# Second-layer keys and values of context batches 2 and 3 made inside the second layer, from a context loaded again

## The reference, cut to what matters

```python
# first layer, on the normed context, with rotation and a bias
kv_in = _layernorm(encoder_output, gamma, beta)
k = kv_in @ Wqkv[D:2*D].T ;  v = kv_in @ Wqkv[2*D:].T ;  q, k = rope(q), rope(k)
attn = softmax(q @ k.T * SCALE + temporal_bias);  attended = attn @ v      # then out, gate, tanh FFN
# second layer, on the raw context
k = ctx @ wk.T + bk ;  v = ctx @ wv.T + bv
attn = softmax(where(mask == 0, -1e9, q @ k.T * 8 ** -0.5)) ;  out = attn @ v   # then wo, 8 experts, top 2
```

## Time and profile before

| what | value |
|---|---|
| median of 3 runs | 558.69 us (555.54 to 559.5) |
| profiled execution | 558.84 us, its span 557.2 us |
| PE busy | 508.0 us (91%), 6338 matmuls |
| ACT busy | 434.7 us (78%) |
| DVE busy | 280.2 us (50%) |
| POOL busy | 169.0 us (30%) |
| mean granted TensorE clock | 0.977 |
| DMA | 74.53 MB, mean 134 GB/s |
| chain that ended last | PE 53%, ACT 12%, DVE 10%, issue 9%, POOL 8%, DMA 5% |

### The profile page before, as it was taken

How to read it: one execution, slowest core, us unless ns; L and a number is a source line. 1 busy time by engine, 2 the same in 40 slices (tenths; PEclk the granted TensorE clock), 3 DMA queues, 4 the chain that set the end, 5 groups by cost and what they waited for, 6 DMA issues and landing times.

```text
span 557.2 us, 15361 instructions
## 1 busy us (share of the span) xinstructions
PE 508.0 (91%) x6338; PEld 260.7 (47%) x6338; DVE 280.2 (50%) x739; ACT 434.7 (78%) x496; POOL 169.0 (30%) x202
## 2 busy tenths in 40 slices
PE   7788998999899898998999999899899989998995
PEld 4444545445445454554555444344443444443343
DVE  5858566874776356653522342336243533440354
ACT  1257486787678787888998999899989998999832
POOL 4468637584785308840110001000000000000000
PEclk9789899999899999999999999999999999999996
DMA  8579885389558314580745291249123910000000
GB/s 269 160 230 288 225 273 138 129 283 292 148 192 285 124 49 126 197 261 17 140 105 188 69 211 40 87 113 223 33 65 76 235 32 8 6 1 2 6 6 16
DMA packets 51584, 74.53 MB, mean 134 GB/s; under 512 B 11146, under 2 KB 40050, under 8 KB 51506
## 3 DMA queue, kind: packets, MB, share of 16 engines
q1 hardware_dynamic: 40258, 37.54, 26.9%
q0 software_dynamic: 5632, 24.07, 12.9%
q10 hardware_dynamic: 5616, 11.86, 7.0%
HBM read 39.95 MB, written 18.83 MB: 106 GB/s over the span
## 4 chain that ended last, share of the span: by engine, by line
PE 53%; ACT 12%; DVE 10%; issue 9%; POOL 8%; DMA 5%; ACTq 1%; SPq 1%; DVEq 0%; POOLq 0%
PE ps L539 24%; PE ps L515 16%; ACT probs L1171 7%; DVE k_swapped L1480 2%; DMA q_side<-in_far_q 2%; PE ps L669 2%; ACT ctx_turned L1171 2%; PE ps L440 2%; DMA ctx_tokens<-in_ctx_rows 2%; DVE row_stats L1442 1%; POOL k L1025 1%; PE ps L450 1%; ACT ctx_tokens L1171 1%; DVE k_parts L1497 1%; POOL k L1023 1%
## 5 line engine op out<-in xcount | busy, mean ns | idle before, releaser
L1171 ACT ACTIVATE probs<-ps 124x1024 f32<-124x1024 f32 (+1 forms) x305 | 295.7, 1024 | 54.2 <-PE ps L520 41.1
L515 PE MATMUL ps<-q_side,k_side 64*124 64x256 bf16 (+1 forms) x1664 | 159.9, 291 | 20.9 <-ACT probs L1171 12.1
L539 PE MATMUL ps<-probs,values 124*9 124x256 f32 (+1 forms) x2440 | 163.7, 383 | 0.0
L515 PEld LDWEIGHTS ps<-q_side,k_side 64*124 64x124 bf16 (+1 forms) x1664 | 80.0, 131 | 124.7 <-ACT probs L1171 62.0
L539 PEld LDWEIGHTS ps<-probs,values 124*9 124x9 f32 (+1 forms) x2440 | 52.9, 90 | 65.6 <-issue 15.5
L1054 POOL TENSOR_TENSOR post_rstd<-post_rstd,power 128x2 f32<-128x2 f32 x12 | 8.5, 712 | 194.0 <-DVE post_rstd L1695 126.5
L520 PE MATMUL ps<-bias_near,bias_w 64*124 64x84 bf16 (+1 forms) x416 | 42.5, 200 | 0.0
L1171 ACT ACTIVATE ctx_tokens<-ps 124x1024 f32<-124x1024 f32 (+1 forms) x37 | 37.9, 1026 | 4.9 <-PE ps L515 4.0
L1480 DVE SCALAR_TENSOR_TENSOR k_swapped<-ps,beta_products,k_table_sb 32x496 f32<-32x496 f32 (+2 forms) x64 | 40.4, 632 | 0.9
L1171 ACT ACTIVATE ctx_turned<-ps 124x1024 f32<-124x1024 f32 (+1 forms) x37 | 37.9, 1024 | 3.4 <-PE ps L515 2.4
L1171 ACT ACTIVATE ctx_normed<-ps 124x1024 f32<-124x1024 f32 (+1 forms) x37 | 37.9, 1025 | 2.4 <-PE ps L515 1.6
(11 more groups left out here) (256 smaller groups left out, 621.0 us busy)
## 6 DMA issues: line engine op xcount, KB each, us to landing
k_side<-k_scratch SPq DMA_DIRECT2D x24, 400.2 KB, 7.8
k_scratch<-k_parts POOLq DMA_DIRECT2D x16, 372.0 KB, 5.4
k_side<-k_parts SPq DMA_DIRECT2D x45, 124.0 KB, 2.5
q_side<-q_parts SPq DMA_DIRECT2D x63, 64.0 KB, 2.7
v_scratch<-values POOLq DMA_DIRECT2D x4, 936.0 KB, 10.9
values<-v_scratch SPq DMA_DIRECT2D x4, 936.0 KB, 14.4
v_scratch<-v POOLq DMA_DIRECT2D x12, 288.0 KB, 5.8
mask_q<-in_mask POOLq DMA_DIRECT2D x8, 400.5 KB, 4.4
```

Of the source, the lines that this page charges most:

```text
L515: last = pe.matmul(ps[0:width, bank, SQ * i:SQ * (i + 1)], kst[rows, j % 2, 2 * g + i, at], qst[rows, query_slot(j, run), 2 * g + i, :], s ...
L539: last = pe.matmul(ps[32 * i:32 * i + VC, ACC + g // 2, SQ * (g % 2):SQ * (g % 2) + SQ], v[0:rows, j % 2, t, h, :], probs_of(u)[0:rows, SQ ...
L1171: act.activation(probs_of(u)[0:rows, :], ps[0:rows, s:s + 2, :].rearrange("p a n -> p (a n)"), ACT.Exp)\
```

## The change

For context batches 2 and 3 (`LATE_FROM` = 2) attention batches 1 and 2 make only the layer-1 keys and values. Each chunk then has one value step, of up to four tiles, in HIGH, and VectorE rounds the high key part before it takes the values out. The layer-2 keys and values of these two batches are made in attention batches 4, 5 and 6, at the slots of `second_keys_at`, from a context that ScalarE's queue loads again (`load_turned_again`, 800 KB, at units (3, 12) and (5, 19)). All of their rounding is VectorE's; SP stores them and loads them back: the keys in two parts, the last chunk's part behind its own store. `VALUES_AT` is changed for batches 4, 5 and 6 (batch 7 keeps the default), two expert steps move from slots 20 and 22 to 22 and 24, and the exps' fifth buffer is the layer-1 key buffer and no longer the turned context.

```diff
+LATE_FROM = 2
+def key_steps(b, n):
+    return KEY_STEPS[n] if b < LATE_FROM else 2
...
+def second_keys_at(j, slot):
+    chunks = {NB: {32: (4, "k1v1"), 36: (5, "k1"), 40: (5, "v1"), 48: (6, "k1"), 50: (6, "v1")},
+              NB + 1: {14: (3, "k1"), 16: (3, "v1"), 28: (4, "k1v1"), 32: (5, "k1"), 36: (5, "v1"), 48: (6, "k1"), 50: (6, "v1")},
+              NB + 2: {14: (3, "k1"), 16: (3, "v1")}}
...
-             NB: (2, 0, 3, 3, 0, 3, 3, 0, 3, 1, 3, 0, 3, 1, 3, 2, 3, 2, 3, 2, 2, 0, 3, 1, 3, 3)}
+             NB: (2, 0, 3, 3, 0, 3, 3, 0, 3, 1, 3, 0, 3, 1, 3, 2, 2, 2, 2, 2, 1, 1, 3, 2, 3, 4),
+             NB + 1: (2, 0, 3, 3, 1, 0, 3, 2, 1, 3, 3, 2, 2, 2, 2, 2, 1, 1, 1, 2, 3, 2, 3, 2, 2, 4),
+             NB + 2: (2, 0, 3, 3, 1, 0, 3, 2, 1, 3, 3, 2, 3, 1, 3, 1, 3, 0, 3, 1, 3, 1, 3, 1, 3, 3)}
...
-    steps = (8, 10, 20, 22, 34, 38, 42, 46)
+    steps = (8, 10, 22, 24, 34, 38, 42, 46)
...
+                    if b >= LATE_FROM:
+                        return
                     fill(HIGH, "k1", b, n)
...
+                elif b >= LATE_FROM:
+                    fill(HIGH, "v", b, n)
+                    one_layer_values(HIGH, n, 0).then_inc(made[HIGH], 1)
...
+            def one_layer_values(bank, n, layer):
+                for i, t in enumerate(range(*CHUNKS[n])):
+                    r = rows_of(t)
+                    last = pe.matmul(ps[0:r, bank, D * i:D * i + D], ct[:, TS * t:TS * t + r], wvv[:, layer, :], start=True, stop=True)
+            def second_layer_keys(b, n, what):
+                pe.wait_ge(ct_late_in, 16 * (b - LATE_FROM + 1))
+                if "k1" in what:
+                    fill(HIGH, "k1", b, n)
+                    pe.matmul(ps[:, HIGH, 0:k_1 - k_0], wk1[:], ct[:, k_0:k_1], start=True, stop=True).then_inc(made[HIGH], 1)
+                if "v1" in what:
+                    fill(LOW, "v1", b, n)
+                    one_layer_values(LOW, n, 1).then_inc(made[LOW], 1)
...
 # SP, in batches 5 and 6, for the batch after
-                    load_second_keys(j + 1, range(len(TERMS)))
+                    if j == NB:
+                        load_second_keys(j + 1, range(len(TERMS)))
+                    else:
+                        store_late(j - NB + 1, 2)
+                        load_late_keys(j + 1, 0)
+                        store_late(j - NB + 1, 3)
+                        load_late_keys(j + 1, 1)
                     load_second_values(j + 1)
+                    if j < NJ - 2:
+                        store_late(j - NB + 2, 0)
...
                 load_shift(j + 1)
+                if NB <= j < NJ - 2:
+                    store_late(j - NB + 2, 1)
...
 # VectorE
             def rest_of_keys(b, n):
+                if b < LATE_FROM: ...
+                else:
+                    high_part(b, n)
+                    first_layer_values(b, n)
                 middle_part(b, n)
...
 # in choose(b), after the third gate step
+                if later:
+                    second_layer_keys(*later)
+                    second_layer_values(*later)
...
 # in the loop over batches 3 to 7
+                    if j < NJ - 1:
+                        second_layer_parts(j - NB + 1, 3)
                 if looks:
                     look_at_mask(looks[1])
+                later = j - NB + 2 if NB <= j < NJ - 2 else None
                 if j < NJ - 1:
-                    for c in range(2):
-                        sample_maxima(j + 1, c)
+                    sample_maxima(j + 1, 0)
+                    if later:
+                        second_layer_keys(later, 0)
+                        second_layer_values(later, 0)
+                        second_layer_parts(later, 0)
+                    sample_maxima(j + 1, 1)
+                    if later:
+                        second_layer_keys(later, 1)
                     make_shift(j + 1)
+                    if later:
+                        second_layer_values(later, 1)
+                        second_layer_parts(later, 1)
...
                     weigh(j - NB - 1, 1)
+                if later:
+                    second_layer_keys(later, 2)
+                    second_layer_values(later, 2)
                 copy_sums(j)
+                if later:
+                    second_layer_parts(later, 2)
```

More of the change, by code:

```diff
@@ L113, in keys_at @@
     for at, (b, n) in first.items():
-        if slot - at in KEY_OFFSETS[:KEY_STEPS[n]]:
+        if slot - at in KEY_OFFSETS[:key_steps(b, n)]:
             return b, n, KEY_OFFSETS.index(slot - at)
     return None
+def second_keys_at(j, slot):
+    chunks = {NB: {32: (4, "k1v1"), 36: (5, "k1"), 40: (5, "v1"), 48: (6, "k1"), 50: (6, "v1")},
+              NB + 1: {14: (3, "k1"), 16: (3, "v1"), 28: (4, "k1v1"), 32: (5, "k1"), 36: (5, "v1"), 48: (6, "k1"), 50: (6, "v1")},
+              NB + 2: {14: (3, "k1"), 16: (3, "v1")}}
+    if slot not in chunks.get(j, {}):
+        return None
+    m, what = chunks[j][slot]
+    return *divmod((j - NB + 1) * NC + m, NC), what
 def sample_at(j):
@@ L686, in beside @@
                     keys(*keys_at(j, slot))
+                if second_keys_at(j, slot) is not None:
+                    second_layer_keys(*second_keys_at(j, slot))
                 if j + 1 < NJ and slot in sample_at(j):
@@ L843, in load_second_keys, with load_late_keys, store_late @@
                 load_keys(sp, G, 1, b, j % 2, k1_in, terms)
+            def load_late_keys(j, half):
+                b = j - NB
+                sp.wait_ge(k1_in, QL * (b + half))
+                if half and b > LATE_FROM:
+                    sp.wait_ge(k1_rest_in, QL * (b - LATE_FROM))
+                for s in range(2):
+                    sp.wait_ge(k1_late_out[s], 16 * (2 * (b - LATE_FROM) + max(half, 1 - s) + 1))
+                cut = CHUNK_KEYS[3][0]
+                load_keys(sp, G, 1, b, j % 2, (k1_in, k1_rest_in)[half], keys=((0, cut), (cut, SK))[half])
+            def store_late(b, n):
+                m, s = late_chunk(b, n), n % 2
+                (t0, t1), (k_0, k_1) = CHUNKS[n], CHUNK_KEYS[n]
+                if m >= 2:
+                    sp.wait_ge(k1_late_out[s], 16 * (m // 2))
+                    sp.wait_ge(v1_late_out[s], 16 * (m // 2))
+                sp.wait_ge(seen[LOW], side.of(LOW, "v1", b, n))
+                sp.dma_start(G["v_dram"][1, b, :, t0:t1], v1s[:, s, 0:t1 - t0]).then_inc(v1_late_out[s], 16)
+                sp.wait_ge(lo1, NC * b + n + 1)
+                sp.dma_start(G["k_dram"][1, b, :, :, k_0:k_1], kp1[:, s, :, 0:k_1 - k_0]).then_inc(k1_late_out[s], 16)
             def load_second_values(j):
@@ L1310, in scalar_program @@
                     key = keys_at(*divmod(u - lag, UB))
-                    if key is not None and key[2] == 0:
+                    if key is not None and key[2] == 0 and key[0] < LATE_FROM:
                         part(*key[:2])
@@ L1525, in both_values, with first_layer_values @@
                 last.then_inc(seen[bank], 1)
+            def first_layer_values(b, n):
+                t0, t1 = CHUNKS[n]
+                if n == 0:
+                    dve.wait_ge(probs_used, UB * (b - 1))
+                    dve.wait_ge(v0_out, 16 * (b - 1))
+                dve.wait_ge(made[HIGH], side.of(HIGH, "v", b, n))
+                for p0, p1 in ((t0, t1),) if t1 < KT else ((t0, KT - 1), (KT - 1, KT)):
+                    r, nt = rows_of(p1 - 1), p1 - p0
+                    at = D * (p0 - t0)
+                    product = ps[0:r, HIGH, at:at + D * nt].rearrange("p (t h d) -> p t h d", h=H, d=HD)
+                    last = dve.tensor_tensor(v[0:r, b % 2, p0:p1, :, 0:HD], product,
+                                             rs[0:r, b % 2, p0:p1].unsqueeze(2).unsqueeze(3).broadcast_to((r, nt, H, HD)), ALU.mult)
+                last.then_inc(seen[HIGH], 1)
@@ new lines, in second_layer_values @@
+            def second_layer_values(b, n):
+                m, s = late_chunk(b, n), n % 2
+                t0, t1 = CHUNKS[n]
+                if m < 2:
+                    dve.wait_ge(v1_out[s], 16 * LATE_FROM * NC // 2)
+                else:
+                    dve.wait_ge(v1_late_out[s], 16 * (m // 2))
+                dve.wait_ge(made[LOW], side.of(LOW, "v1", b, n))
+                for p0, p1 in ((t0, t1),) if t1 < KT else ((t0, KT - 1), (KT - 1, KT)):
+                    r, nt = rows_of(p1 - 1), p1 - p0
+                    at = D * (p0 - t0)
+                    product = ps[0:r, LOW, at:at + D * nt].rearrange("p (t h d) -> p t h d", h=H, d=HD)
+                    last = dve.tensor_copy(v1s[0:r, s, p0 - t0:p1 - t0, :, 0:HD], product)
+                last.then_inc(seen[LOW], 1)
@@ new lines, in second_layer_keys @@
+            def second_layer_keys(b, n):
+                m, s = late_chunk(b, n), n % 2
+                w = CHUNK_KEYS[n][1] - CHUNK_KEYS[n][0]
+                if m < 2:
+                    dve.wait_ge(k1_out[s], 16 * LATE_FROM * NC // 2)
+                else:
+                    dve.wait_ge(k1_late_out[s], 16 * (m // 2))
```

(5 more changed lines are left out.)

84 lines of the change are left out of this document (61 added, 23 removed).

## The result

| | before | after |
|---|---|---|
| median | 559.32 us (555.54 to 562.34, 20 runs) | 562.72 us (559.15 to 569.99, 20 runs) |
| ratio | | 1.006, 95% interval 1.0038 to 1.0082 |
| profiled span | 557.2 us | 561.3 us |

The change makes the kernel slower by 0.6%, 3.4 us. I had forecast 1.0 us faster, 557.8.

What follows compares the result with a forecast made beforehand. The prediction took TensorE to bound layer 1, with TensorE and ScalarE within 2 us of each other in layer 2. Layer 1 gave -15.1 and layer 2 +14.1: -1.0 on 558.84, so 557.8 us, range 550.5 to 566.

Steps and rivals of the forecast that it cites:

- batch 1, up to pair 15: Layer 1: work, waits and a slow clock removed, against 4.0 us for a new wait with slow clock; batch total -7.1.
- batch 1, far queries ("just enough"): End of batch 1: the DMA chain gets 5 to 7 us earlier, just enough for PE's earlier arrival; no cost.
- batch 2: Layer 1: 6.0 us of work, a wait of 1.40 and smaller waits of 0.6 go; -8.0.
- batch 3, context reload ("nothing"): The 800 KB load at unit 12 has ten times its landing until it is used; no cost.
- batch 4, pairs 16 to 25: Floor 24.5, mask wait and scores ahead 3.4, slow clock 1.5, small losses 0.5: 29.9 us, or +7.5.
- batch 5, pairs 7 to 25: Floor 44.0, a 1.3 us wait at the small chunk, 0.8 of earlier losses left: 46.1 us, or +5.5.
- last rival: Batch 1 doesn't get shorter, since far queries land where they did behind other loads; +6.5, 564.3 us; chance 0.05.
- Both batches are PE's, so all of it is on the path: Batches 1 and 2: TensorE bounds both, so the 6.0 us of work removed in each counts fully.
- forecast wait of 2.6 us and its slow clock (4.0): Batch 1, keys of chunk 3: PE waits 2.6 us for VectorE's rotation of chunk 2, plus 1.4 for slow clock.
- 1.3 for the slow clock of before: Batch 1: the slow clock behind the old 1.95 us wait goes, gaining 1.3 us.
- rival of the side banks: Layer 2: LOW and HIGH become the bound, refills waiting for VectorE in fixed order; +8, 565.8 us; chance 0.22.
- first rival: Batch 1's rotation wait is absent, batch 4's mask wait covered or without slow clock; 550.3 us; chance 0.26.

Runs made afterwards that it cites:

- e2_far: Changed kernel, with the far queries of batch 1's last tiles issued ahead of the 800 KB load of the context's deviations; 560.28 us, ratio 1.003.
- e3_ctx: Changed kernel, with the reload of context 2 issued at unit 40 of batch 3 instead of unit 12; 559.42 us, ratio 1.0018.
- e12_split: Changed kernel with five reorderings, plus batch 2's value steps of the two middle chunks cut in two over neighbouring pairs; 554.87 us, ratio 0.9949.
- e5_before_orders: Kernel before the change, with batch 4's second mask piece behind the second sample's maxima and far queries ahead of the row statistics load; 556.6 us, ratio 0.9956.
- e1_mask: Changed kernel, with VectorE reducing batch 4's second mask piece behind the second sample's maxima; 558.82 us, ratio 0.9985.
- e4_three: Changed kernel with the edits of e1_mask, e2_far and e3_ctx together; 554.81 us, ratio 0.9953.
- e9_less: e4_three, with each late layer-2 value pass making only its first tile, the other three left out; 552.51 us, ratio 0.9911.
- e7_sample: e4_three, with VectorE reading the first-layer values ahead of the high key rounding in the last chunk of contexts 2 and 3; 555.29 us, ratio 0.9929.

## Why the forecast went wrong

In us, by the prediction's own terms (per batch, profiled executions):

| step | forecast | measured |
|---|---|---|
| batch 1, up to pair 15 | -11.1 + 4.0 | -8.8, a wait of 0.95 in it |
| batch 1, sample for VectorE | 0 | +1.8 |
| batch 1, far queries ("just enough") | 0 | +3.7 |
| batch 2 | -8.0 | -6.0 |
| batch 3, context reload ("nothing") | 0 | +1.0 |
| batch 4, pairs 16 to 25 | +7.5 | +8.8 |
| batch 5, pairs 7 to 25 | +5.5 | +6.5 |
| batch 6 and 7 | +1.1 | +1.6 |
| sum of batches 1 to 7 | -1.0 | +8.6 |

The prediction counted batches 4 and 5 from pair to pair, and so does this table. From first exp to first exp batch 4 shows +7.6 and batches 6 and 7 +2.8, because the last pairs of batches 4 and 5, each 1.2 us longer with four value units and a side step, come behind the next batch's first exp and are counted with the batch after.

**The step that failed** is the one on the far queries of batch 1: "Three chunks at 1.5 to 2.5 us earlier is 5 to 7, just enough". The issue did come 6.9 us earlier and the landing 6.5, but PE was there 8.2 us earlier: at 177.4, where the 2.09 us of wait begin, and at 185.5 before, where it already waited 0.4. I compared the DMA chain's gain with the total of the batch and took the equality for cover, and I kept the landing at 10.6 us without pricing a miss. The miss of 2.09 us cost 4.2 against e2_far's 8.0 for pairs 22 to 24, 3.7 against before, since the slow clock follows. My last rival has this place and a wrong reason: it wanted the far queries to land where they had landed, for +6.5, at 0.05. e2_far shows that the order behind an 800 KB load was enough. This step is the largest of the misses but not the whole: forecast and sum lie 9.6 us apart, and the terms below make up the rest.

**The same fault in batch 3**: I asked whether the reload would be in time for its own readers (it was: it landed at 272.7 and is first read some 70 us later) and not which small loads it would pass through the DMA engines with. e3_ctx shows the 1.0 us.

**Batch 2, and 0.6 us of batch 1**: the work taken out was sized well, pair by pair: pairs that lost a value step fell by 1.05 (1.06 in the earlier trace rows), the key step without its second pass by 0.81 (0.85). What was wrong was "Both batches are PE's, so all of it is on the path". With the value step gone a pair lasts 1.66 us, under ScalarE's two exps, and the next is longer by 0.57; three such places (pairs 9, 12 and 16) make 1.7 of the 2.0 missing in batch 2, and the one at pair 16 the 0.6 of the 1.8 in batch 1's row that is no wait for VectorE. e12_split shows the cause. I had used the pace of ScalarE for layer 2 and not for layer 1.

**Batch 1's side bank**: the forecast wait of 2.6 us and its slow clock (4.0) was 0.95 without one. I had left the row statistics where the earlier trace rows have them; they moved forward with the faster VectorE. The 1.3 for the slow clock of before was no gain by itself, as e5_before_orders shows; what went was VectorE's hold on pairs 10 to 12, from 12.9 to 7.6 us. This error had the other sign. It was partly refilled by the sample's wait, a place that I had not looked at.

**Layer 2 in size.** Pairs 16 to 25 of batch 4 took 31.2 us where I had 29.9. The mask's wait and what follows it took 5.5 (e1_mask) and not 4.9, and the rest 25.7 (e4_three) and not 25.0. Batches 4 to 7 together are 11.4 us longer without the mask's wait (e4_three), where I counted 9.2: there was less slack to hide in than I allowed, in batch 5 above all, and no run shows in which of its pairs. The rival of the side banks is not the reason: besides the mask's wait the only one for a side bank in layer 2 is the 0.81 us of batch 5, where I had allowed 1.3.

**Right**: batch 4 in its mechanism (e1_mask). The prices of side work: e9_less gave back 2.0 of 2.1. The cast's fall to 0.42 us: L1497 in the earlier trace rows starts at 148.03, beside GpSimd's L1029 (147.95 to 149.07), and ends 0.3 us behind it. All large casts of this line that took 1.3 us, in before and for context 1 in after, have such a subtraction beside them, and those of contexts 2 and 3 in after have none. The Trainium skill (SBUF, State Buffer, "two separate sides") says that VectorE and GpSimd lock one shared port pair for a whole instruction; the trace agrees, with 1.32 against 0.42. SP's stores and loads of late keys cost nothing: PE waits for none of them in batches 5 to 7. The stores that went are 372 + 288 = 660 KB a chunk and not 580, which no term used. The range's lower end of 550.5 did not quite take in the first rival's 550.3.

**What stays open.** The profiled batches 1 to 7 add 8.6 us, batch 0 and the tail take 4.7 off by chance, and the first exp comes 0.3 later, so that the spans differ by 4.1; the ratio says 3.4 over all runs. The profiled execution of after lies 1.7 us over the kernel's own median span. That does not tell what the slow clock costs in a usual run: of the other kernels with the mask wait e2_far lies 3.0 over its median and e3_ctx 3.6, but of those without it e1_mask lies 1.0 under and e12_split 5.7 over. There is one trace of each kernel.

## What to carry to other kernels

When a change lets an engine arrive earlier, list for each of its later waits both times, that of the arrival and that of the release, and subtract: a chain that gets faster by nearly the same amount covers nothing, and a small load issued behind a large one is the first to miss. Price a miss with what the clock can do behind it, here 0 to 2.4 us more. And apply the cheap reorderings that repair a change to the kernel before as well: here they gave it 0.4% by themselves (interval 0.1 to 0.75%), and what the repaired change adds to that (e7_sample, at most 0.3%) lies within the intervals.
